# Three banks for single heads' scores, three for maxima, and products of values in two groups a tile

## The chip, the cores and the metric

The kernel runs on one core of one Trainium2 chip. The core has five engines that run their own instruction streams and meet only at semaphores: TensorE (PE, with its weight loads listed as PEld), VectorE (DVE), ScalarE (ACT), GpSimd (POOL) and SyncE (SP), which here issues the DMAs. TensorE writes to the accumulation memory PSUM, eight banks of 128 partitions by 512 float32. The metric is the device time of the whole program in microseconds; lower is better.

## The reference

Four cross-attention layers follow one another. Layer 0 has 16 heads of 64 and a bias; layers 1 to 3, which the change touches, have 16 query heads of 32, four key/value heads shared by four query heads each, and a root-mean-square norm ahead of the queries. Inputs are float32, 8 batches of 512 rows of 512, with 512 context rows of 1024.

```
xn   = x * rsqrt(mean(x*x) + 1e-5) * norm_w
q    = xn @ wq                          # 512 rows, 16 heads of 32
k, v = ctx @ wk, ctx @ wv               # 512 rows, 4 heads of 32
for each head h, with its k and v head g = h // 4:
    p      = softmax(q[h] @ k[g].T / sqrt(32))      # 512 x 512
    o[h]   = p @ v[g]
x    = x + concat(o) @ wo
```

## The kernel before, in words

The program first projects keys and values of all layers, then runs layer 0, then layers 1 to 3 in `grouped_layers`, from about 2150 us to the end. There the work is 24 batches `it` (three layers by eight batches) of four tiles `t`, 96 tiles in all. A tile is one key/value head with its four query heads. For each tile TensorE does the following, by the names used in this text:

- **M0 to M15**, `maximum`, line 2014: 16 products of 128 queries by 512 keys, one bank each, of which DVE takes a row maximum (`reduce_max`, line 1882). They work up to two tiles ahead (`LEAD = 22`). The banks are 4 and 5 in turn, so each waits until the one two before it is reduced.
- **T**, `turn`, line 2036: four transposes that turn the maxima of the next tile, from which ACT writes four rows into the query operand (`shift`, line 1766, in two halves of two instructions).
- **S0 to S7**, `scores`, line 2045: two products each, for two heads (here x.0 and x.1), into banks 0 and 1 or 2 and 3. ACT takes both banks in one instruction (`exponential`, line 1775, here **E0 to E7**) into `probs`.
- **O0 to O3**, `outputs`, line 2059: products of the exponentials with the values, for 128 keys and four heads. Four matmuls of 32 columns each stand side by side in the array; all accumulate in bank 6.
- **D**, `denominators`, lines 2073 and 2078: two sets of the same form with a matrix of ones, in bank 7. POOL adds E2 to E5 to the first ones beforehand (line 1684).
- **Q0 to Q3**, `project_q`, line 2003, and **P0 to P3**, `project_out`, line 2085: three full products each, for the queries three tiles ahead and for the output of the batch before, both in bank 7.

Once a batch, at t = 3, TensorE also sums squares for the batch after next (`sum_squares`, line 1989, here **SS**, bank 7), DVE inverts the mean square and ACT takes its root at t = 1 (`inv_rms`, line 1752, between two table loads).

The order on every engine is written out by hand in its `batch` function, and each engine keeps it. ACT has in every tile E0, rounding of an output, the taking of outputs and denominators, E1, E2, E3, rounding of q, E4, E5, E6, first half of `shift`, E7, second half. TensorE's S0 waits for the first half of `shift`, D for the second (`shifted`). `take_q` (line 1877) is DVE's reading of bank 7 after Q3, between the reductions of M5 and M6; SS and P0 wait for it (`q_taken`). The order of a tile on TensorE stands in the function `batch` below.

Of the kernel before, what the change touches and what calls it, by code (L numbers as in the profile page):

```python
# [5 lines left out]
P = 128  # L6
# [17 lines left out]
KT = S // P  # L24
# [1394 lines left out]
def grouped_layers(nc, name, x_out, k_scratch, v_scratch, wq, wo, shared, norm_w):  # L1419
# [16 lines left out]
    FIRST_TURNB = 3  # L1436

    with ExitStack() as mem:
# [93 lines left out]

        def max_bank(i):
            return 4 + i % 2
# [33 lines left out]
        def _(sp):  # L1568
# [41 lines left out]
            def batch(it, par):  # L1610
# [8 lines left out]
                for t in range(T):  # L1619
                    if there(it, t + AHEAD):  # L1620
                        wait(sp, scored, tile_no(it, t) * NS)
                        load_k(*at(it, t + AHEAD))
                    if there(it, t - LAG):
                        load_residual(it, t)
                    if there(it, t - LAG - 1):
                        store(it, t - 1)
                    if t == 1 and there(it, 2 * T):
                        sp.wait_ge(x_split, (it + 2) * CK)
                        load_x(it + 2)
                    if t == 1 and there(it, T):  # L1630
# [33 lines left out]
        def _(pool):  # L1664
# [14 lines left out]
            def sum_probs(it, t, n):  # L1679
# [3 lines left out]
                pool.wait_ge(exped, g * NS + n + 1)  # L1683
# [43 lines left out]
        def _(act):  # L1727
# [42 lines left out]
            def exponential(it, t, n):  # L1770
                g = tile_no(it, t)
                act.wait_ge(scored, g * NS + n + 1)
                if n < 2:
                    wait(act, summed, (g - 1) * SUMS + n + 1)
                act.activation(probs[:, n], ps[:, 2 * (n % 2):2 * (n % 2) + 2, :], ACT.Exp).then_inc(exped, 1)  # L1775
# [67 lines left out]
        def _(dve):  # L1843
# [41 lines left out]
            def maximum(it, t, i):  # L1885
                t_m, n = max_target(it, t, i)
                if there(it, t_m):
                    reduce_max(tile_no(it, t) * M + LEAD + i, t_m, n, max_bank(i))
# [96 lines left out]
        def _(pe):  # L1985
# [31 lines left out]
            def maximum(it, t, i):  # L2017
                t_m, n = max_target(it, t, i)
                if there(it, t_m):
                    no = tile_no(it, t) * M + LEAD + i  # L2020
                    pe.wait_ge(reduced, no - 1)
                    one_maximum(*at(it, t_m), n, max_bank(i))
# [16 lines left out]
            def scores(it, t, n):  # L2039
# [3 lines left out]
                wait(pe, exped, g * NS + n - 1)  # L2043
                for j in range(2):
                    last = pe.matmul(bank(2 * (n % 2) + j), k_ops[:, s, kt * P:(kt + 1) * P], q_ops[:, s, 2 * hp + j, :],  # L2045
                                     start=True, stop=True)
                last.then_inc(scored, 1)

            def outputs(it, t, kt, par):
# [7 lines left out]
                pe.wait_ge(exped, g * NS + (kt + 1) * (H // 2))  # L2057
# [48 lines left out]
            def batch(it, par):  # L2106
                for t in range(T):
                    scores(it, t, 0)
                    maximum(it, t, 0)
                    outputs(*at(it, t - 1), KT - 1, par if t > 0 else 1 - par)  # L2110
# [14 lines left out]
                    outputs(it, t, 0, par)  # L2125
# [16 lines left out]
                    maximum(it, t, 11)  # L2142
                    outputs(it, t, 1, par)
                    turn(*at(it, t + 1))
                    scores(it, t, 6)
                    maximum(it, t, 12)
# [3 lines left out]
                    outputs(it, t, 2, par)  # L2150
# [7 lines left out]
            for no in range(LEAD):  # L2158
                wait(pe, reduced, no - 1)
                one_maximum(0, no // M, no % M, max_bank(no))  # L2160
                if no == M + 1:
                    pe.wait_ge(reduced, M)
                    for q in range(QT):
# [69 lines left out]
```

## Time and profile before

| what | us |
|---|---|
| median of 3 runs (lowest to highest) | 4220.01 (4219.65 to 4222.34) |
| the profiled execution | 4216.71 |
| its span in the trace | 4214.9 |
| PE busy in the span | 4068.2 |
| DVE busy | 2468.1 |
| ACT busy | 2074.4 |
| first instruction of the 96 tiles' maxima (L2014) | 2172.8 |
| last O of the trace (L2059) | 4195.2 |

All durations in this text are from the one profiled execution. The rows of the timeline give the start and the length of an instruction or of a run of equal ones; on TensorE a matmul is listed for about 0.40 us although the next one starts 0.23 us later, so its pace is read from start to start, and a bracket for idle time shows only what exceeds that overlap. The chain of waits shows each piece with what it adds to the path.

### The profile page before, as it was taken

To read this page: it belongs to the slowest core of one execution; us is meant where nothing else is said; L and a number is where in the kernel's file an instruction comes from. 1 tells how busy PE (TensorE), PEld (TensorE's weight loads), DVE (VectorE), ACT (ScalarE), POOL (GpSimd) and SP (SyncE) were. 2 spreads that over 40 slices of the span, in tenths; PEclk is the share of its full clock that TensorE was granted. 3 is DMA by queue.
4 is the path that set the end of the run, shared out by engine and by line. 5 is a ranking of instruction groups with operands and counts; after the bars stand their busy time and mean duration, and the time that the engine had idled before them with its cause. 6 is when DMAs were issued, how large, how long until landed. Compare 5 with 4: busy or idle time off the path is not lost. (4 is left out here: it accounts for less than half of the span.)

```text
span 4214.9 us, 52271 instructions
## 1 busy us (share of the span) xinstructions
PE 4068.2 (97%) x19496; PEld 2639.1 (63%) x19496; DVE 2468.1 (59%) x3453; ACT 2074.4 (49%) x2648; POOL 2000.2 (47%) x1072
## 2 busy tenths in 40 slices
PE   9999999997999999999969999999999999999999
PEld 7888888885556665666544555555555555555555
DVE  3122300013665556555658778777877887788775
ACT  3111211122444445434427666776676677666665
POOL 0000000003565556555626676667666766676666
PEclk9999999998999999999979999999999999999999
DMA  5333522234455445545533333333333333333322
GB/s 185 130 135 135 173 79 83 88 100 118 131 128 134 122 130 130 133 122 133 128 91 84 88 86 86 96 96 97 83 95 90 86 98 93 94 89 88 93 79 65
DMA packets 316070, 452.01 MB, mean 107 GB/s; under 512 B 45176, under 2 KB 117368, under 8 KB 315832
## 3 DMA queue, kind: packets, MB, share of 16 engines
q1 hardware_dynamic: 315832, 448.86, 37.9%
q8 instruction: 147, 2.41, 0.2%
q14 instruction: 91, 0.75, 0.1%
HBM read 217.72 MB, written 102.77 MB: 76 GB/s over the span
## 5 line engine op out<-in xcount | busy, mean ns | idle before, releaser
L1882 DVE TENSOR_REDUCE a_max_cols<-a_ps 128x1 f32<-128x512 f32 x1536 | 1018.1, 673 | 322.6 <-PE a_ps L2014 316.4
L1775 ACT ACTIVATE a_probs<-a_ps 128x1024 f32<-128x1024 f32 x768 | 784.7, 1025 | 602.7 <-PE a_ps L2045 597.4
L2014 PE MATMUL a_ps<-a_k_ops,a_q_ops 96*128 96x512 f32 x1536 | 652.1, 436 | 50.3 <-DVE a_max_cols L1882 33.3
L1684 POOL TENSOR_TENSOR a_sums<-a_probs 128x1024 f32<-128x1024 f32 x192 | 456.1, 2392 | 321.7 <-ACT a_probs L1775 320.5
L1036 DVE TENSOR_REDUCE a_max_cols<-a_ps 128x1 f32<-128x512 f32 x522 | 346.1, 686 | 342.8 <-PE a_ps L1189 342.8
L2014 PEld LDWEIGHTS a_ps<-a_k_ops,a_q_ops 96*128 96x128 f32 x1536 | 291.3, 190 | 396.4 <-DVE a_max_cols L1882 219.1
L2045 PE MATMUL a_ps<-a_q_ops,a_k_ops 128*128 128x512 f32 x1536 | 492.7, 402 | 1.5 <-ACT a_q_ops L1766 0.9
L803 POOL MEMSET a_ident<- 128x128 f32 x1 | 0.2, 204 | 974.9 <-issue 974.9
L1684 POOL TENSOR_TENSOR a_sums<-a_sums,a_probs 128x1024 f32<-128x1024 f32 x192 | 454.0, 2387 | 0.0
L2059 PE MATMUL a_ps<-a_probs,a_v 128*32 128x512 f32 x3072 | 410.1, 606 | 0.9 <-ACT a_probs L1775 0.9
L303 DVE TENSOR_TENSOR cp_c_lo<-cp_raw,cp_c_hi 128x1024 fp32r<-128x1024 f32 x64 | 78.4, 1225 | 527.7 <-ACT cp_c_hi L247 527.7
L1901 DVE RECIPROCAL a_stage<-a_stage 128x128 f32<-128x128 f32 x384 | 361.2, 942 | 13.7 <-ACT a_stage L1787 13.7
L948 ACT ACTIVATE a_probs<-a_ps 128x1024 f32<-128x1024 f32 x256 | 257.0, 1024 | 142.7 <-PE a_ps L1213 133.1
L2045 PEld LDWEIGHTS a_ps<-a_q_ops,a_k_ops 128*128 128x128 f32 x1536 | 284.0, 190 | 57.4 <-issue 7.2
L826 POOL TENSOR_TENSOR a_sums<-a_sums,a_probs 128x1024 f32<-128x1024 f32 x128 | 311.1, 2430 | 10.0
L1213 PE MATMUL a_ps<-a_q_ops,a_k_ops 128*128 128x512 f32 x1024 | 289.4, 405 | 14.2 <-ACT a_probs L948 13.6
L411 PE MATMUL cp_ps<-cp_w_hi,cp_c_lo 128*128 128x512 f32 (+1 forms) x768 | 285.3, 371 | 0.0
L411 PE MATMUL cp_ps<-cp_w_lo,cp_c_hi 128*128 128x512 f32 (+1 forms) x768 | 285.2, 371 | 0.0
L411 PE MATMUL cp_ps<-cp_w_hi,cp_c_hi 128*128 128x512 f32 (+1 forms) x768 | 285.1, 371 | 0.0
L392 PE MATMUL cp_ps<-cp_c_hi,cp_w_hi 128*128 128x512 f32 x704 | 275.5, 391 | 8.9 <-DVE cp_w_lo L297 8.9
L392 PE MATMUL cp_ps<-cp_c_hi,cp_w_lo 128*128 128x512 f32 x704 | 275.1, 391 | 0.0
L392 PE MATMUL cp_ps<-cp_c_lo,cp_w_hi 128*128 128x512 f32 x704 | 275.1, 391 | 0.0
(131 smaller groups left out, 7182.0 us busy)
## 6 DMA issues: line engine op xcount, KB each, us to landing
a_k_ops<-k_scratch SPq DMA_DIRECT2D x201, 256.0 KB, 4.1
a_q_ops<-a_qn_hi SPq DMA_DIRECT2D x768, 64.0 KB, 2.0
k_scratch<-cp_out SPq DMA_DIRECT2D x88, 512.0 KB, 2.8
a_q_ops<-a_qn_hi SPq DMA_DIRECT2D x268, 128.0 KB, 2.3
cp_raw<-in_ctx_t SPq DMA_DIRECT2D x64, 512.0 KB, 4.1
x_raw<-out_t SPq DMA_DIRECT2D x25, 1024.0 KB, 7.1
a_q_ops<-a_qn_lo SPq DMA_DIRECT2D x384, 64.0 KB, 2.0
a_x_res<-out_t SPq DMA_DIRECT2D x92, 256.0 KB, 3.1
```

What stands on the lines that cost most here:

```text
L392: done = pe.matmul(ps[:, m % BANKS, :], w[:, k, n * P:(n + 1) * P], c[par][:, k, :], start=(k == 0 and i == 0), stop=(k == KC - 1 and i == 2))
L411: done = pe.matmul(ps[:, v_bank(n), 0:w], c[par][:, k, t * P:(t + 1) * P], v[:, k, c0:c0 + w], start=(k == 0 and i == 0), stop=(k == KC - ...
L826: pool.tensor_tensor(sums[:, hp], (probs if i == 1 else sums)[:, hp], probs[:, n], ALU.add)\
L1036: dve.tensor_reduce(max_cols[:, t % 2, col:col + 1], bank(max_bank(p)), AX.X, ALU.max, negate=True).then_inc(reduced, 1)
L1213: last = pe.matmul(bank(2 * (n % 2) + j), k_ops[:, s, k_head(h), p, kt * P:(kt + 1) * P], q_ops[:, s, h, p, :], start=(p == 0), stop=(p == ...
L1684: pool.tensor_tensor(sums[:, hp], (probs if n < H else sums)[:, hp], probs[:, n], ALU.add)\
L1775: act.activation(probs[:, n], ps[:, 2 * (n % 2):2 * (n % 2) + 2, :], ACT.Exp).then_inc(exped, 1)
L1882: dve.tensor_reduce(max_cols[:, t % 2, col:col + 1], bank(b), AX.X, ALU.max, negate=True)\
L1901: dve.reciprocal(part, part).then_inc(recip_done, 1)
L2014: pe.matmul(bank(b), q_ops[0:SHIFT, s, h, q * P:(q + 1) * P], k_ops[0:SHIFT, s, :], start=True, stop=True).then_inc(smax, 1)
L2045: last = pe.matmul(bank(2 * (n % 2) + j), k_ops[:, s, kt * P:(kt + 1) * P], q_ops[:, s, 2 * hp + j, :], start=True, stop=True)
L2059: last = pe.matmul(ps[h * d:(h + 1) * d, OUTB, :], v[:, par, kt, t * d:(t + 1) * d], probs[:, kt * (H // 2) + h // 2, h % 2, :], start=(kt ...
```

## The change

In `grouped_layers` alone:

- The scores of a head go into one of three banks (0 to 2) in turn, head by head. A product of head number i, counted on through the tiles, waits until the exponential of head i - 3 is done. Before, both products of S(n) waited for E(n-2), both heads of it.
- The exponential is one instruction a head (512 columns) in place of one for two heads (1024 columns). `scored` and `exped` count heads.
- The maxima use banks 3, 4 and 5 in turn, so that each waits for the one three before it.
- O2 moves from between M14 and M15 to the next tile, right ahead of O3. O0 moves from between M6 and M7 to right ahead of O1. M12 moves ahead of S6.
- The first turn uses bank 2 and waits for the first queries' taking.

The diff, cut to its core:

```
-    FIRST_TURNB = 3
+    FIRST_TURNB = 2
+    SCORE_BANKS = MAX_BANKS = 3
...
+        def score_bank(g, n, j):
+            return (2 * (g * NS + n) + j) % SCORE_BANKS
         def max_bank(i):
-            return 4 + i % 2
+            return SCORE_BANKS + i % MAX_BANKS
...
             def exponential(it, t, n):
                 g = tile_no(it, t)
-                act.wait_ge(scored, g * NS + n + 1)
                 if n < 2:
                     wait(act, summed, (g - 1) * SUMS + n + 1)
-                act.activation(probs[:, n], ps[:, 2 * (n % 2):2 * (n % 2) + 2, :], ACT.Exp).then_inc(exped, 1)
+                for j in range(2):
+                    act.wait_ge(scored, 2 * (g * NS + n) + j + 1)
+                    act.activation(probs[:, n, j, :], bank(score_bank(g, n, j)), ACT.Exp).then_inc(exped, 1)
...
             def maximum(it, t, i):
-                    pe.wait_ge(reduced, no - 1)
-                    one_maximum(*at(it, t_m), n, max_bank(i))
+                    pe.wait_ge(reduced, no - MAX_BANKS + 1)
+                    one_maximum(*at(it, t_m), n, max_bank(no))
...
             def scores(it, t, n):
-                wait(pe, exped, g * NS + n - 1)
                 for j in range(2):
-                    last = pe.matmul(bank(2 * (n % 2) + j), k_ops[:, s, kt * P:(kt + 1) * P], q_ops[:, s, 2 * hp + j, :],
-                                     start=True, stop=True)
-                last.then_inc(scored, 1)
+                    wait(pe, exped, 2 * (g * NS + n) + j + 1 - SCORE_BANKS)
+                    pe.matmul(bank(score_bank(g, n, j)), k_ops[:, s, kt * P:(kt + 1) * P], q_ops[:, s, 2 * hp + j, :],
+                              start=True, stop=True).then_inc(scored, 1)
...
                     maximum(it, t, 0)
+                    outputs(*at(it, t - 1), KT - 2, par if t > 0 else 1 - par)
                     outputs(*at(it, t - 1), KT - 1, par if t > 0 else 1 - par)
...
                     maximum(it, t, 6)
-                    outputs(it, t, 0, par)
...
                     maximum(it, t, 11)
+                    outputs(it, t, 0, par)
                     outputs(it, t, 1, par)
                     turn(*at(it, t + 1))
+                    maximum(it, t, 12)
                     scores(it, t, 6)
-                    maximum(it, t, 12)
                     maximum(it, t, 13)
                     scores(it, t, 7)
                     maximum(it, t, 14)
-                    outputs(it, t, 2, par)
                     maximum(it, t, 15)
```

Three places show how instructions move. Line numbers of the changed kernel are 5 or 6 higher: L2020 is M, L2051 is S, L2064 is O, L2078 and L2083 are D, L1995 is SS, L1781 is E and L1771 is `shift`.

TensorE, the end of a tile, before: S7, M14, O2, M15, the next tile's S0, M0, O3 and the first set of D.

```order
L2045 MATMUL a_ps<-a_q_ops,a_k_ops 128x512 [waits a1_exped]
L2045 MATMUL a_ps<-a_q_ops,a_k_ops 128x512
L2014 MATMUL a_ps<-a_k_ops,a_q_ops 128x512 [waits a1_reduced]
L2059 MATMUL a_ps<-a_probs,a_v 32x512 [waits a1_exped]
L2059 MATMUL a_ps<-a_probs,a_v 32x512 x3
L2014 MATMUL a_ps<-a_k_ops,a_q_ops 128x512 [waits a1_reduced]
L2045 MATMUL a_ps<-a_q_ops,a_k_ops 128x512 [waits a1_exped,a1_shifted]
L2045 MATMUL a_ps<-a_q_ops,a_k_ops 128x512
L2014 MATMUL a_ps<-a_k_ops,a_q_ops 128x512 [waits a1_reduced]
L2059 MATMUL a_ps<-a_probs,a_v 32x512 [waits a1_exped]
L2059 MATMUL a_ps<-a_probs,a_v 32x512 x3
L2073 MATMUL a_ps<-a_probs,a_ones 32x512 [waits a1_shifted]
```

The same place in the changed kernel: S6, M13, S7, M14, M15, the next tile's S0, M0, O2, O3, the first set of D.

```order
L2051 MATMUL a_ps<-a_q_ops,a_k_ops 128x512 [waits a1_exped] x2
L2020 MATMUL a_ps<-a_k_ops,a_q_ops 128x512 [waits a1_reduced]
L2051 MATMUL a_ps<-a_q_ops,a_k_ops 128x512 [waits a1_exped] x2
L2020 MATMUL a_ps<-a_k_ops,a_q_ops 128x512 [waits a1_reduced] x2
L2051 MATMUL a_ps<-a_q_ops,a_k_ops 128x512 [waits a1_exped,a1_shifted]
L2051 MATMUL a_ps<-a_q_ops,a_k_ops 128x512 [waits a1_exped]
L2020 MATMUL a_ps<-a_k_ops,a_q_ops 128x512 [waits a1_reduced]
L2064 MATMUL a_ps<-a_probs,a_v 32x512 [waits a1_exped]
L2064 MATMUL a_ps<-a_probs,a_v 32x512 x3
L2064 MATMUL a_ps<-a_probs,a_v 32x512 [waits a1_exped]
L2064 MATMUL a_ps<-a_probs,a_v 32x512 x3
L2078 MATMUL a_ps<-a_probs,a_ones 32x512 [waits a1_shifted]
```

Eight full matmuls now stand between the start of S6.0 and S0.1 without a set of O among them, and S0.1 has a wait of its own.

ACT, the end of tile t = 1, before: E4, E5, E6, a half of `shift`, E7, the other half, the next tile's E0.

```order
L1775 ACTIVATE a_probs<-a_ps 128x1024 [waits a1_scored] x3
L1766 ACTIVATE a_q_ops<-a_ps 1x512 [waits a1_turned]
L1766 ACTIVATE a_q_ops<-a_ps 1x512
L1775 ACTIVATE a_probs<-a_ps 128x1024 [waits a1_scored]
L1766 ACTIVATE a_q_ops<-a_ps 1x512 [waits a1_turned]
L1766 ACTIVATE a_q_ops<-a_ps 1x512
L1775 ACTIVATE a_probs<-a_ps 128x1024 [waits a1_summed,a1_scored]
```

The same in the changed kernel.

```order
L1781 ACTIVATE a_probs<-a_ps 128x512 [waits a1_scored] x6
L1771 ACTIVATE a_q_ops<-a_ps 1x512 [waits a1_turned]
L1771 ACTIVATE a_q_ops<-a_ps 1x512
L1781 ACTIVATE a_probs<-a_ps 128x512 [waits a1_scored] x2
L1771 ACTIVATE a_q_ops<-a_ps 1x512 [waits a1_turned]
L1771 ACTIVATE a_q_ops<-a_ps 1x512
L1781 ACTIVATE a_probs<-a_ps 128x512 [waits a1_scored,a1_summed]
L1781 ACTIVATE a_probs<-a_ps 128x512 [waits a1_scored]
```

The order is the same, with two instructions in place of each exponential.

TensorE, the middle of tile t = 3, before: S3, M6, O0, SS, M7.

```order
L2045 MATMUL a_ps<-a_q_ops,a_k_ops 128x512 [waits a1_exped]
L2045 MATMUL a_ps<-a_q_ops,a_k_ops 128x512
L2014 MATMUL a_ps<-a_k_ops,a_q_ops 128x512 [waits a1_reduced]
L2059 MATMUL a_ps<-a_probs,a_v 32x512 [waits a1_exped,a1_out_taken]
L2059 MATMUL a_ps<-a_probs,a_v 32x512 x3
L1989 MATMUL a_ps<-a_sq,a_ones 128x512 [waits a1_sq_step,a1_q_taken]
L2014 MATMUL a_ps<-a_k_ops,a_q_ops 128x512 [waits a1_reduced]
```

The same in the changed kernel, and on to S4 and M8.

```order
L2051 MATMUL a_ps<-a_q_ops,a_k_ops 128x512 [waits a1_exped] x2
L2020 MATMUL a_ps<-a_k_ops,a_q_ops 128x512 [waits a1_reduced]
L1995 MATMUL a_ps<-a_sq,a_ones 128x512 [waits a1_sq_step,a1_q_taken]
L2020 MATMUL a_ps<-a_k_ops,a_q_ops 128x512 [waits a1_reduced]
L2051 MATMUL a_ps<-a_q_ops,a_k_ops 128x512 [waits a1_exped] x2
L2020 MATMUL a_ps<-a_k_ops,a_q_ops 128x512 [waits a1_reduced]
```

SS now follows M6 at once. In the 96 tiles ACT issues 1536 exponentials in place of 768; the other engines issue the same instructions as before.

## Rows read from the trace of the kernel before

**Rows 1.** The page: busy us, share of the span and instructions by engine.
```profile
PE 4068.2 (97%) x19496; PEld 2639.1 (63%) x19496; DVE 2468.1 (59%) x3453; ACT 2074.4 (49%) x2648; POOL 2000.2 (47%) x1072
```

**Rows 2.** By window: length, busy us of PE, PEld, DVE, ACT, POOL, granted clock, DMA.
```profile
3116.57:3137.11 20.54, 20.45 (x109) 11.63 (x108) 17.86 (x27) 14.55 (x19) 13.68 (x7) 1.00 0.30 71
...
3158.24:3178.66 20.42, 20.33 (x110) 11.69 (x109) 15.05 (x22) 14.36 (x18) 14.75 (x9) 1.00 0.34 90
```

**Rows 3.** The chain of waits in tile 2: start, length, what.
```profile
3161.11 0.86 PE a_ps L2078 x8
...
3167.51 0.23 PE a_ps L2014
3167.74 1.00 PE a_ps L2059 x8
3168.74 0.43 PE a_ps L2014
```

**Rows 4.** Timeline, end of tile 2: start, length, engine, operation, count, idle before.
```profile
3175.18 0.70 PE L2045 MATMUL a_ps<-a_q_ops,a_k_ops 128*128 128x512 f32 x2
...
3175.92 1.03 ACT L1775 ACTIVATE a_probs<-a_ps 128x1024 f32<-128x1024 f32 x1 [2.49 <-PE a_ps L2045]
...
3176.18 0.63 PE L2045 MATMUL a_ps<-a_q_ops,a_k_ops 128*128 128x512 f32 x2
...
3176.89 0.49 PE L2014 MATMUL a_ps<-a_k_ops,a_q_ops 96*128 96x512 f32 x1
3176.97 1.18 ACT L1766 ACTIVATE a_q_ops<-a_ps 1x512 fp32r<-1x512 f32 x2
...
3177.32 1.07 PE L2059 MATMUL a_ps<-a_probs,a_v 128*32 128x512 f32 x8
...
3178.17 1.02 ACT L1775 ACTIVATE a_probs<-a_ps 128x1024 f32<-128x1024 f32 x1
...
3179.22 1.19 ACT L1766 ACTIVATE a_q_ops<-a_ps 1x512 fp32r<-1x512 f32 x2
...
3180.46 1.07 PE L2073 MATMUL a_ps<-a_probs,a_ones 128*32 128x512 f32 x8
...
3181.35 1.04 PE L2078 MATMUL a_ps<-a_sums,a_ones 128*32 128x512 f32 x8
```

**Rows 5.** Timeline, middle of tile 1.
```profile
3141.83 0.63 PE L2045 MATMUL a_ps<-a_q_ops,a_k_ops 128*128 128x512 f32 x2
...
3143.53 1.28 ACT L1752 ACT_TABLE_LOAD   x1
...
3144.83 0.63 ACT L1752 ACTIVATE a_inv<-a_ms 128x512 f32<-128x512 f32 x1
...
3146.47 0.62 PE L2045 MATMUL a_ps<-a_q_ops,a_k_ops 128*128 128x512 f32 x2
...
3146.77 1.94 ACT L1775 ACTIVATE a_probs<-a_ps 128x1024 f32<-128x1024 f32 x2
```

**Rows 6.** By source line L1743: count, shortest/median/longest ns, first and last start.
```profile
L1743 ACT ACTIVATE x_hi<-x_raw x46: 1046/1048/1057, 2204.5 to 4053.9; 128x1024 fp32r<-128x1024 f32 x46
```

**Rows 7.** By source line L1738, the same columns.
```profile
L1738 ACT ACTIVATE wq_hi<-a_w_raw x12: 617/620/625, 2300.2 to 3645.8; 128x512 fp32r<-128x512 f32 x12
```

**Rows 8.** Timeline, middle of tile 3.
```profile
3187.76 0.39 PE L2014 MATMUL a_ps<-a_k_ops,a_q_ops 96*128 96x512 f32 x1
3187.89 0.67 DVE L1877 TENSOR_TENSOR a_qf<-a_ps,a_inv 128x512 f32<-128x512 f32 x1
...
3189.07 1.13 PE L1989 MATMUL a_ps<-a_sq,a_ones 128*128 128x512 f32 x2
```

**Rows 9.** Timeline, start of tile 1.
```profile
3137.11 0.63 PE L2045 MATMUL a_ps<-a_q_ops,a_k_ops 128*128 128x512 f32 x2
...
3138.34 0.50 PE L2014 MATMUL a_ps<-a_k_ops,a_q_ops 96*128 96x512 f32 x1 [0.60 <-DVE a_max_cols L1882]
```

**Rows 10.** PE's waits: total us, times, longest us.
```profile
PE a_ps L2014 <- DVE a_max_cols L1882: 33.3, 45, 2.6
```

More of the change, by code:

```diff
@@ L1620, in batch @@
                     if there(it, t + AHEAD):
-                        wait(sp, scored, tile_no(it, t) * NS)
+                        wait(sp, scored, 2 * tile_no(it, t) * NS)
                         load_k(*at(it, t + AHEAD))
@@ L1682, in sum_probs @@
                     pool.wait_ge(summed, g * SUMS + n - H + 1)
-                pool.wait_ge(exped, g * NS + n + 1)
+                pool.wait_ge(exped, 2 * (g * NS + n + 1))
                 pool.tensor_tensor(sums[:, hp], (probs if n < H else sums)[:, hp], probs[:, n], ALU.add)\
@@ L1887, in maximum @@
                 if there(it, t_m):
-                    reduce_max(tile_no(it, t) * M + LEAD + i, t_m, n, max_bank(i))
+                    reduce_max(tile_no(it, t) * M + LEAD + i, t_m, n, max_bank(tile_no(it, t) * M + LEAD + i))
             def split_x(n, k):
@@ L2056, in outputs @@
                     wait(pe, out_taken, g)
-                pe.wait_ge(exped, g * NS + (kt + 1) * (H // 2))
+                pe.wait_ge(exped, 2 * (g * NS + (kt + 1) * (H // 2)))
                 for h in range(H):
@@ L2158, in _ @@
             for no in range(LEAD):
-                wait(pe, reduced, no - 1)
+                wait(pe, reduced, no - MAX_BANKS + 1)
                 one_maximum(0, no // M, no % M, max_bank(no))
@@ L2162, in _ @@
                     pe.wait_ge(reduced, M)
+                    pe.wait_ge(q_taken, AHEAD)
                     for q in range(QT):
@@ L2167, in _ @@
             pairs(pe, batch)
+            outputs(N - 1, T - 1, KT - 2, 1)
             outputs(N - 1, T - 1, KT - 1, 1)
             denominators(N - 1, T - 1)
-            pe.wait_ge(exped, G * NS)
+            pe.wait_ge(exped, 2 * G * NS)
             out_part(T - 1, 0, range(T), 0)
```

## The prediction

> **What bounds the kernel now.** I read the page first. PE is busy for 97% of the span, DVE for 59%, ACT for 49% [rows 1]. The busy times by window then show one batch's tiles of the grouped layers: tile 0 takes 20.54 us and tile 2 20.42, with 20.45 and 20.33 us of PE in them, DVE busy 17.86 and 15.05, ACT 14.55 and 14.36, and the granted clock at 1.00, the 2.4 GHz level [rows 2]. So TensorE's own sequence sets the end there. DVE and ACT have room on average, and what matters is where TensorE waits inside a tile, and what its sequence costs apart from the matmuls. The chain of waits shows the second [rows 3]: a set of O between two Ms adds 1.00 us and the M behind it 0.43, where an M elsewhere adds 0.23 and a set that follows one of its own form 0.86. A change from full to narrow matmuls and back thus costs 0.14 + 0.20 = 0.34 us. The timeline of a tile's end shows the first [rows 4]: M14 starts 0.71 us after the second pair of S instead of 0.47, held by DVE, and the O set 0.43 us after it instead of 0.33, since its load was not hidden.
>
> **The change part by part.** The working is done on tile 2 of one batch and carried to the 96 tiles.
>
> 1. Joined sets. Two of four round trips a tile go, the one of O0 and the one of O2: 2 x 0.34 = 0.68 us. O2 and O3 then stand in front of D, as one narrow stretch.
>
> 2. The end of a tile. S6 starts at 3175.18 and D at 3180.46, 5.28 us [rows 4]. In it ACT is a chain: E6 starts at 3175.92, 0.04 us after S6's end, then half of `shift` at 3176.97 (1.18 us), E7 at 3178.17, the other half at 3179.22, and D begins 0.05 us after that. Before, S0 needed E6 and the first half of `shift`, not E7, and O2 and M15 filled the time. Now S0.1 is three heads behind E7.0, and only M13, S7, M14, M15 and S0.0 stand between S6 and it: eight steps of 0.23, 1.87 us. ACT's chain from M12 on, the first after the transposes, where S6 now starts 0.31 us later (S6's first pair: 0.70 less 0.39 [rows 4]): 0.31 + 0.39 (S6.0) + 0.04 + 1.09 (E6, both heads) + 0.02 + 1.18 + 0.02 + 0.60 (E7.0) + 0.05 = 3.70 us. Then S0.1 with an unhidden load 0.34, M0 0.33, O2 0.89 and O3 0.86 (as D's two sets: 3180.46 to 3181.35, and 0.86 [rows 3, 4]) = 2.42. Together 6.12 us where 5.28 stand now: +0.84, in which O2's round trip and M14's wait are already counted as gains. O0's round trip is outside: -0.34. Net +0.50 us a tile, 95 tile ends: +47.5 us. S7.1 waits for E6.0 and S0.0 for the first half of `shift`, both inside this chain. E7.1 and the second half end at 5.4 us of it, ahead of D.
>
> The trace has no exponential of 512 columns. Copies of 1024 and 512 columns take 1.048 and 0.620 us [rows 6, 7], so 512 columns are worth 0.43, and 1.02 - 0.43 = 0.60. Two exponentials in a row take 1.94 us together and so overlap by 0.10 [rows 5]; a pair of halves is 0.49 + 0.60 = 1.09. Bounds: half of 1.02, so the pair at 1.02 and one at 0.51, which takes 0.16 us from each end of a tile (-15 us) and as much from item 3 (-3); or the 0.62 of the copy with no overlap, 1.24 and 0.62, which adds 0.17 (+16) and in item 3 0.2 plus a wait of S4.1 of up to 0.3 (+11). I take 0.60, the nearest row's.
>
> The Trainium skill ("ScalarE: Activation LUTs", "What ACT_TABLE_LOAD costs") gives an ACTIVATE with immediates 186 ns plus 0.833 ns a column and an overlap of 93 ns. By that the half would be 0.61 us and the pair 1.13, an estimate, and the end of a tile 0.05 us later, some 5 us in all. This case's rows show 1.02 for 1024 columns where it would have 1.04, so its fixed part is a little high here. The same section adds about 1.38 us of drain to each table load; by that E2 would start 2.8 us later than the loads alone make it. The trace disagrees, since the instruction behind the 1.28 us load starts 0.02 us after it [rows 5].
>
> 3. Tile 1. After E1 ACT loads a table (1.28 us), takes the root (0.63), and loads the other table (1.28); E2 starts only at 3146.77 [rows 5]. Before, S3 needed E1, and nothing waited. Now S3.1 needs E2.0. From S1 at 3141.83: 0.40 + 0.04 + 1.09 (E1), loads and root with gaps of about 0.05 in all 3.24, E2.0 0.60, 0.05 = 3147.25. S3.1 stood at 3146.70: +0.55, and 0.10 for its unhidden load. +0.65 us in some 20 batches (three layer starts, where another wait hides it, and the last batch, which takes no root, are out): +13 us. S4.1 comes 1.04 us later and E3.0 ends 0.99 us later, so it just passes.
>
> 4. Tile 3. SS waits for `take_q`, which ends at 3187.89 + 0.67 = 3188.56 [rows 8]. Now it follows M6 (3187.76) directly and would start at 3187.99; it starts at 3188.61 instead, 0.62 us late. Before, O0's set covered this; only its round trip was counted as saved. The 22 batches that have it: +13.6 us. P0 waits for the same in other tiles, but 1.2 us after M6 or later, when it is over.
>
> 5. Third bank for maxima. At the start of tile 1 M0 starts 1.23 us after S0, not 0.47, because DVE has the splits of x between its reductions, and the O set after it 0.10 later [rows 9]. M0 now needs only the reduction of M13, which DVE has long done, since S0.1 is late: -0.86 x 23 = -20 us. Of the visible waits of M on DVE, 33.3 us in 45 times [rows 10], about 14 are these; of the other 19, the longest 2.6, the third bank can save the time of one M's spacing each. I take -4, between 0 and -10.
>
> 6. At nothing: one semaphore count more in S and E (the waits are on the matmuls' own instructions); 15% more ACT work, 8 x 0.17 = 1.4 us a tile under about 6 us idle [rows 2]; POOL, which waits for whole pairs as before and whose last sum ends before the turn; SP, whose K loads wait for the same point. If ACT's cover went, each tile would pay up to 1.4 us, but only its chains above are on the path. The prologue's extra wait stands once.
>
> Sum: +47.5 + 13 + 13.6 - 20 - 4 = +50 us. The profiled execution took 4216.7 and becomes 4267; the median of the runs is 3.3 us above that execution, so the runs' median becomes 4270. In words: 65 us of narrow-to-full changes, some 33 of M14's waits and 24 of other DVE waits are saved, and more than that is paid where TensorE now stands at the three-bank limit.
>
> **The rivals.**
>
> A. The waits are covered (the other side, faster). If ACT's chain to S0.1 took no longer than the 1.87 us of matmuls, only gains would be left: joined sets -65, M14's wait and load 0.34 x 95 = -32, D's small wait of about 0.1 -8, M0 and the rest -24, with items 3 and 4 +27: 4118. It turns the sign once the chain to S0.1 is 0.5 us shorter than my 3.70. Against it: `shift` alone is 1.18 us and is unchanged, and with halves at 0.51 the chain is still 3.54. 6%.
>
> B. It balances, 4220: gains of item 5 grow because M12 to M15 run into reductions elsewhere too, or the unhidden loads cost nothing. That needs 0.5 us a tile from waits of which I see 0.34. 8%.
>
> C. ACT is dearer (slower yet): halves do not overlap, because each waits on its own semaphore, and S4.1 waits in tile 1. The upper bound above, 4270 + 27 = 4297. For it: `shift` behind E6 does not overlap (0.02 us of gap). Against: E3 overlaps E2 although it has a wait. 12%.
>
> D. The change does not do what it says: a joined set still costs a full change, and 65 us do not come, 4334. Against it, D's second set at 0.86 us [rows 3]. 2%.
>
> My forecast 72%.
>
> **How the numbers follow.** The forecast's own range is 4250 to 4285, from the lower bound of the exponential and half of the upper. To leave out no more than 2 in 10 it reaches down towards B and up into C: 4236 to 4297. This kernel's measurement tells 0.2%, 8.4 us, from no change. Faster takes A and a part of B: 0.08. Same takes most of B: 0.08. Slower: 0.84.
>
> **What would show it.** In the changed profile: exponentials of 512 columns at 0.60 us; S6 to D at about 5.8 us, and S0's second matmul starting about 0.05 us after an E7.0; tile 1 with S3.1 behind E2.0; SS right behind `take_q`; M0 of tile 1 no longer held by DVE; O sets joined at 0.86; tile 2 at about 20.9 us. It would be wrong if S0.1 is not held by ACT, or if E6 starts earlier than S6.0's end.

## The result, and the profile after

The changed kernel takes 4279.27 us, the median of 4 runs (4276.54 to 4281.31), against 4221.18 us (4219.65 to 4224.85) for the kernel before on the same chip: ratio 1.0134, interval 1.0119 to 1.0149. It is 58 us slower, where the prediction had 50. The profiled execution took 4276.54 us, with a span of 4274.7, 59.8 more than before.

The page of the changed kernel, which answers to [rows 1]: TensorE is busy for a smaller share of a longer span, and ACT has 768 more instructions, the halved exponentials. Further lines of the changed kernel, beside those named above: L1883 is `take_q`, L1888 `reduce_max`, L2042 the transposes T, L2090 the products P.

```profile
PE 4057.1 (95%) x19496; PEld 2657.4 (62%) x19496; DVE 2461.1 (58%) x3453; ACT 2113.5 (49%) x3416; POOL 1997.1 (47%) x1072
```

The waits of PE in the changed kernel (total us, times, longest), which answer to [rows 10]. The row of M on DVE that led before (33.3 us, 45 times) has shrunk to 5.2, and what leads now is S0 waiting for `shift`:

```profile
PE a_ps L2051 <- ACT a_q_ops L1771: 69.0, 95, 1.2
PE a_ps L2051 <- ACT a_probs L1781: 16.3, 29, 1.8
...
PE a_ps L1995 <- DVE a_qf L1883: 10.3, 22, 0.5
...
PE a_ps L2020 <- DVE a_max_cols L1888: 5.2, 8, 1.7
```

The count is the thing to see: 95 times, once at each tile's end, 22 for SS, once a batch. By window, the four tiles of one batch after (from one S0 to the next; columns as in [rows 2]):

```profile
3225.73:3246.84 21.11, 20.27 (x108) 11.84 (x108) 17.55 (x27) 14.93 (x27) 13.25 (x7) 1.00 0.26 66
3246.84:3268.51 21.67, 20.37 (x109) 11.86 (x109) 17.84 (x27) 16.14 (x28) 12.11 (x7) 1.00 0.45 124
3268.51:3289.41 20.90, 20.06 (x108) 11.93 (x109) 14.76 (x23) 14.73 (x26) 14.52 (x9) 1.00 0.32 80
3289.41:3312.09 22.68, 21.36 (x110) 12.23 (x111) 15.85 (x24) 13.16 (x25) 17.11 (x11) 1.00 0.28 72
```

Tiles 0 and 2 were 20.54 and 20.42 [rows 2]. The clock is 1.00 in all four, so nothing of what these tiles lose is the clock's. (From 2250 us to the last batch the trace of the changed kernel has two short stretches at 0.50, at 2302 and at 2998 us, and that of the kernel before has none; by the 1.7 us that such a stretch costs in a run further down, they are worth some 3 us.) Medians over 20 batches each (batches 3 to 22, start of S0 to start of S0), worked out from the starts of all matmuls in both traces:

| tile | before | after | difference |
|---|---|---|---|
| 0 | 20.54 | 21.13 | +0.58 |
| 1 | 21.14 | 21.66 | +0.52 |
| 2 | 20.41 | 20.91 | +0.50 |
| 3 | 21.45 | 22.68 | +1.23 |

Together +2.83 a batch, 68 over 24 batches. Some 8 us of it do not come, mostly in the first two batches, which differ by -1.8 and +1.5 us.

The end of tile 2 in the timeline of the changed kernel, which answers to [rows 4]:

```profile
3286.31 0.48 PE L2020 MATMUL a_ps<-a_k_ops,a_q_ops 96*128 96x512 f32 x1
...
3286.63 0.64 PE L2051 MATMUL a_ps<-a_q_ops,a_k_ops 128*128 128x512 f32 x2
...
3287.07 1.08 ACT L1781 ACTIVATE a_probs<-a_ps 128x512 f32<-128x512 f32 x2 [2.95 <-PE a_ps L2051]
...
3288.18 1.18 ACT L1771 ACTIVATE a_q_ops<-a_ps 1x512 fp32r<-1x512 f32 x2
...
3289.38 1.09 ACT L1781 ACTIVATE a_probs<-a_ps 128x512 f32<-128x512 f32 x2
...
3289.41 1.13 PE L2051 MATMUL a_ps<-a_q_ops,a_k_ops 128*128 128x512 f32 x2 [0.72 <-ACT a_q_ops L1771]
...
3290.70 1.92 PE L2064 MATMUL a_ps<-a_probs,a_v 128*32 128x512 f32 x16
...
3292.45 1.04 PE L2078 MATMUL a_ps<-a_probs,a_ones 128*32 128x512 f32 x8
```

Read it from the back. O2 and O3 are one run of 16 (1.92). S0's two matmuls take 1.13 us together instead of 0.63, since the second waits for E7.0. S0 starts at 3289.41, 0.05 us after the first half of `shift` ends at 3289.36, where TensorE would have been ready 0.9 us earlier. From M12 to D are 6.14 us. The chain of waits of that tile says the same in pieces:

```profile
3286.79 0.26 PE a_ps L2051
...
3287.07 1.08 ACT a_probs L1781 x2
...
3288.18 0.58 ACT a_q_ops L1771
...
3288.77 0.59 ACT a_q_ops L1771
...
3289.38 0.61 ACT a_probs L1781
```

In the kernel before, the path of the same tile leaves TensorE once, between S6 and M14, for one reduction:

```profile
3176.15 0.70 DVE a_max_cols L1882
```

In the changed kernel it leaves TensorE at S6.0's end for E6, both instructions of the first half of `shift`, and E7.0, which ends at 3289.99: nearly 3 us at the tile's end.

### The profile page after: what moved, and what is told of

Its sections match the earlier page's. It is cut to its first block, busy times and chain, and to the rows that moved or that the text cites. A ratio compares the mean times of both kernels' runs of the same rounds, so it can differ in the third digit from the quotient of the medians.

```text
span 4274.7 us, 53040 instructions
## 1 busy us (share of the span) xinstructions
PE 4057.1 (95%) x19496; PEld 2657.4 (62%) x19496; DVE 2461.1 (58%) x3453; ACT 2113.5 (49%) x3416; POOL 1997.1 (47%) x1072
## 4 chain that ended last, share of the span: by engine, by line
PE 37%; ACT 9%; DVE 3%; issue 1%; SPq 0%; POOL 0%; DMA 0%; ACTq 0%; DVEq 0%
PE a_ps L2064 8%; PE a_ps L2090 6%; PE a_ps L2020 6%; PE a_ps L2051 6%; ACT a_probs L1781 5%; PE a_ps L2009 4%; ACT a_q_ops L1771 3%; PE a_ps L2083 2%; PE a_ps L2078 2%; PE a_ps L2042 1%; DVE a_max_cols L1888 1%; PE a_ps L1995 1%; ACT L1781 1%; ACT L1757 1%; DVE a_qf L1883 0%
## 5 line engine op out<-in xcount | busy, mean ns | idle before, releaser
L1888 DVE TENSOR_REDUCE a_max_cols<-a_ps 128x1 f32<-128x512 f32 x1536 | 998.3, 671 | 409.8 <-PE a_ps L2020 405.4
L1781 ACT ACTIVATE a_probs<-a_ps 128x512 f32<-128x512 f32 x1536 | 830.6, 598 | 577.6 <-PE a_ps L2051 563.5
L2051 PE MATMUL a_ps<-a_q_ops,a_k_ops 128*128 128x512 f32 x1536 | 555.8, 421 | 96.7 <-ACT a_q_ops L1771 69.0
L2020 PE MATMUL a_ps<-a_k_ops,a_q_ops 96*128 96x512 f32 x1536 | 614.2, 421 | 14.2 <-DMA a_q_ops<-a_qn_hi 8.6
L1036 DVE TENSOR_REDUCE a_max_cols<-a_ps 128x1 f32<-128x512 f32 x522 | 346.1, 686 | 342.9 <-PE a_ps L1189 342.9
L2051 PEld LDWEIGHTS a_ps<-a_q_ops,a_k_ops 128*128 128x128 f32 x1536 | 291.1, 190 | 285.1 <-ACT a_probs L1781 126.0
L2020 PEld LDWEIGHTS a_ps<-a_k_ops,a_q_ops 96*128 96x128 f32 x1536 | 292.9, 191 | 156.7 <-issue 87.7
L2064 PE MATMUL a_ps<-a_probs,a_v 128*32 128x512 f32 x3072 | 370.8, 600 | 0.0
L948 ACT ACTIVATE a_probs<-a_ps 128x1024 f32<-128x1024 f32 x256 | 257.0, 1024 | 142.7 <-PE a_ps L1213 133.2
L1213 PE MATMUL a_ps<-a_q_ops,a_k_ops 128*128 128x512 f32 x1024 | 289.5, 405 | 14.2 <-ACT a_probs L948 13.6
L1704 POOL TENSOR_TENSOR a_a_lo<-a_stage,a_a_hi 128x512 fp32r<-128x512 f32 x96 | 122.3, 1274 | 363.0 <-ACT a_a_hi L1797 363.0
```

Of the source, the lines that this page charges most:

```text
L1036: dve.tensor_reduce(max_cols[:, t % 2, col:col + 1], bank(max_bank(p)), AX.X, ALU.max, negate=True).then_inc(reduced, 1)
L1213: last = pe.matmul(bank(2 * (n % 2) + j), k_ops[:, s, k_head(h), p, kt * P:(kt + 1) * P], q_ops[:, s, h, p, :], start=(p == 0), stop=(p == ...
L1781: act.activation(probs[:, n, j, :], bank(score_bank(g, n, j)), ACT.Exp).then_inc(exped, 1)
L1888: dve.tensor_reduce(max_cols[:, t % 2, col:col + 1], bank(b), AX.X, ALU.max, negate=True)\
L2020: pe.matmul(bank(b), q_ops[0:SHIFT, s, h, q * P:(q + 1) * P], k_ops[0:SHIFT, s, :], start=True, stop=True).then_inc(smax, 1)
L2051: pe.matmul(bank(score_bank(g, n, j)), k_ops[:, s, kt * P:(kt + 1) * P], q_ops[:, s, 2 * hp + j, :], start=True, stop=True).then_inc(score ...
```

## The experiments

Theory 1 is the account of the prediction: the new order puts TensorE at the three-bank limit behind ACT's chain at the tile's end, and takes the cover away elsewhere. Theory 2, the rival, puts the loss to the number of banks for scores and holds the new order by itself to be a gain. Times are medians of four executions (of nine or ten in three of the runs); the ratio is to the kernel before, measured together with that run.

### The two halves of the change

**Order alone** (the kernel before with its own banks and exponentials, and the changed order on TensorE):

```
                     maximum(it, t, 0)
+                    outputs(*at(it, t - 1), KT - 2, par if t > 0 else 1 - par)
...
                     maximum(it, t, 6)
-                    outputs(it, t, 0, par)
...
                     maximum(it, t, 11)
+                    outputs(it, t, 0, par)
                     outputs(it, t, 1, par)
                     turn(*at(it, t + 1))
+                    maximum(it, t, 12)
                     scores(it, t, 6)
-                    maximum(it, t, 12)
...
                     maximum(it, t, 14)
-                    outputs(it, t, 2, par)
```

> Only the order of the change on TensorE, with the four score banks, two maximum banks and whole exponentials of before. Theory 1 (cover at the tile's end: with O2 gone from there, ACT's chain E6, half of shift stands open): S0.0 waits for the half of shift at 3.25 us after M12, D comes 5.9 us after M12 (6.1 in the changed kernel), no wait of S3 in tile 1, M0 of tile 1 again held by DVE: about 4266 us. Theory 2 (three banks for heads are the cost, joined sets only a gain): the joined sets save 65 us and nothing is lost, about 4160.

Measured: 4324.17 us, ratio 1.0248 [1.0230, 1.0266]. The direction is Theory 1's, and Theory 2 is out. But the size was missed by 58 us. With two banks the order puts Ms close together that O sets kept apart. The timeline in the middle of tile 2 of this kernel (M is L2014 here):

```profile
3303.15 0.77 PE L2014 MATMUL a_ps<-a_k_ops,a_q_ops 96*128 96x512 f32 x2
3303.28 0.68 DVE L1877 TENSOR_TENSOR a_qf<-a_ps,a_inv 128x512 f32<-128x512 f32 x1
...
3303.87 1.97 DVE L1882 TENSOR_REDUCE a_max_cols<-a_ps 128x1 f32<-128x512 f32 x3
...
3304.61 0.50 PE L2014 MATMUL a_ps<-a_k_ops,a_q_ops 96*128 96x512 f32 x1 [0.21 <-DVE a_max_cols L1882]
```

M6 and M7 stand together, DVE has `take_q` ahead of their reductions, and M8 waits for M6's. Over the span this is 64.0 us of M on DVE (131 times) in place of 33.3. Besides, of 20 tiles 1 (batches 3 to 22) ten took 23.4 us and eight 21.7. A stretch at the granted clock 0.50 lies in each of the long ones and in none of the short ones, so it costs 1.7 us. With 13 such stretches from 2250 us to the last batch, 22 us, and the 31 us of M on DVE, this makes some 53 of the 58, an estimate.

**Banks and exponentials alone** (the changed kernel with the order of before):

```
-                    outputs(*at(it, t - 1), KT - 2, par if t > 0 else 1 - par)
...
                     maximum(it, t, 6)
+                    outputs(it, t, 0, par)
...
                     maximum(it, t, 11)
-                    outputs(it, t, 0, par)
                     outputs(it, t, 1, par)
                     turn(*at(it, t + 1))
+                    scores(it, t, 6)
                     maximum(it, t, 12)
-                    scores(it, t, 6)
...
                     maximum(it, t, 14)
+                    outputs(it, t, 2, par)
```

> Only the banks and the exponentials by heads, in the order of before (O0 behind M6, O2 between M14 and M15, M12 behind S6). Theory 1: O2 covers ACT's chain, S0.1 waits no more than 0.05 us, M14's wait and tile 1's M0 wait are gone, S3.1 in tile 1 still waits for E2.0: about 4194 us, less than before. Theory 2: three banks cost wherever S stands, 4240 to 4280.

Measured: 4193.81 us, 0.9937 [0.9919, 0.9955], as forecast. This half makes the kernel faster. A tile's end in its timeline:

```profile
3242.47 0.70 PE L2051 MATMUL a_ps<-a_q_ops,a_k_ops 128*128 128x512 f32 x2
...
3245.63 0.82 PE L2051 MATMUL a_ps<-a_q_ops,a_k_ops 128*128 128x512 f32 x2
...
3247.65 1.06 PE L2078 MATMUL a_ps<-a_probs,a_ones 128*32 128x512 f32 x8
```

S6 to D is 5.18 us; it was 5.28 [rows 4] and is 5.82 in the changed kernel (3286.63 to 3292.45). S0.1 starts 0.31 us after S0.0 here (median), where the pace is 0.23 and the changed kernel has 0.62.

**Which banks.** Three kernels change only the numbers in `SCORE_BANKS, MAX_BANKS`: 4, 2 and 3, 2 in the changed order, and 4, 2 in the order of before.

```
-    SCORE_BANKS = MAX_BANKS = 3
+    SCORE_BANKS, MAX_BANKS = 4, 2
```

> The changed kernel with four banks for heads and two for maxima, all else the same. Theory 1: S0.0's wait for the half of shift stays (3.08 us after M12), only E7.0's wait of 0.3 us goes; S3.1 in tile 1 waits no more (-0.75 a batch), M0 in tile 1 waits for DVE again (+0.9): about 4254 us. Theory 2: the three-bank limit was the cost, about 4160 to 4200.

> The changed kernel with two banks for maxima instead of three (one bank unused). The joined sets covered DVE too: behind M6 and between M14 and M15 five maxima now follow closely. From the run with four and two banks (4337 us) and the limit of three heads, which adds 0.3 us a tile end and 0.75 in tile 1: about 4350 to 4385 us, and a granted clock under 1 in tile 1. Rival (the two-bank runs were slow for another cause, the four banks): about 4300.

> The order of before, with exponentials by heads in four banks and two banks for maxima: of the banks' change only the split of the exponential. Theory 1: the split is worth nothing by itself, about 4218 us; the 27 us of the banks alone are the third bank for maxima (M14's 0.35 us a tile and tile 1's 0.86) less S3.1's wait. Rival: the split itself gains, since E starts one matmul earlier: 4195 to 4205.

| order on TensorE | scores, maxima | us | ratio [interval] |
|---|---|---|---|
| changed | 3, 3 | 4279.27 | 1.0134 [1.0119, 1.0149] |
| changed | 4, 2 | 4336.80 | 1.0270 [1.0251, 1.0288] |
| changed | 3, 2 | 4350.86 | 1.0306 [1.0289, 1.0324] |
| before | 3, 3 | 4193.81 | 0.9937 [0.9919, 0.9955] |
| before | 4, 2 | 4225.65 | 1.0008 [0.9998, 1.0018] |
| before | 4, 2, E not halved (kernel before) | 4221.18 | 1 |

The first was a miss for both theories (4254, and 4160 to 4200): a fourth bank for scores, bought with the third for maxima, makes it slower by 58 us. The other two came out as expected. Halved exponentials alone are worth nothing that can be measured. That is a balance: by the starts of all matmuls tile 0 is 0.84 us longer than in the kernel before, since M15 comes 1.48 us after the last matmul of O2 and not 0.52, and tiles 1, 2 and 3 are 0.37, 0.11 and 0.10 shorter. The third bank for maxima is worth 32 us in the order of before, together with heads in three banks (4225.65 to 4193.81), and 72 in the changed order (4350.86 to 4279.27). The rows do not add up over the orders: order and bank are tied through DVE. The timeline of the 4, 2 kernel at the start of tile 1 shows what the bank covers:

```profile
3281.84 1.81 DVE L1898 TENSOR_TENSOR x_lo<-x_raw,x_hi 128x512 fp32r<-128x512 f32 x1
...
3284.30 0.50 PE L2020 MATMUL a_ps<-a_k_ops,a_q_ops 96*128 96x512 f32 x1 [1.70 <-DVE a_max_cols L1888]
...
3285.51 0.79 PE L2020 MATMUL a_ps<-a_k_ops,a_q_ops 96*128 96x512 f32 x1 [0.24 <-DVE a_max_cols L1888]
...
3286.23 3.15 PE L2064 MATMUL a_ps<-a_probs,a_v 128*32 128x512 f32 x16
```

M15 waits 1.70 us for a reduction behind DVE's splits of x (L1898). And the joined O sets take 3.15 us, not 1.92. The windows of the same kernel (the whole of tile 1, then two pieces of it) show why: the granted clock falls to 0.50, the 1.2 GHz level, in the first piece, by its mean of 0.68 about 1.3 us before the piece's end. M0, which starts just then and is listed with 0.79 us and not 0.50, and the O sets behind it run at that level.

```profile
3284.64:3307.69 23.05, 22.00 (x109) 12.07 (x107) 17.36 (x27) 15.42 (x27) 11.59 (x6) 0.93 0.37 110
3284.64:3286.64 2.00, 1.76 (x8) 0.68 (x10) 2.00 (x5) 1.94 (x5) 0.00 (x0) 0.68 0.48 115
3286.64:3288.64 2.00, 2.00 (x12) 0.39 (x8) 1.21 (x3) 1.07 (x3) 0.85 (x1) 0.50 0.57 151
```

From 2250 us to the last batch the lower level was granted for some 78 us in the 4, 2 kernel, in the order-alone kernel for some 44 and in the 3, 2 kernel for some 31. At the 1.7 us of a stretch that the order-alone kernel showed, this is an estimated 39, 22 and 15 us.

### The terms of the sum, one by one

Each takes the changed kernel and undoes one thing.

**O2 back** between M14 and M15:

```
-                    outputs(*at(it, t - 1), KT - 2, par if t > 0 else 1 - par)
...
                     maximum(it, t, 14)
+                    outputs(it, t, 2, par)
```

> The changed kernel with O2 alone put back between M14 and M15; it costs a round trip of 0.34 us a tile. Theory 1: the set fills the wait, S0.1 at 3.72 us after M12 hardly waits, D is held by the second half of shift at 5.4 us instead of 6.1: -0.7 a tile, about 4211 us. Theory 2 (the end of a tile was not held by ACT): +0.34 a tile, about 4310.

Measured: 4210.45 us, 0.9975 [0.9965, 0.9985], as forecast. Tile 2 takes 20.22 in place of 20.91. This one move of eight narrow matmuls is 69 us, more than the whole loss.

**The first half of `shift` ahead of E6:**

```
-                    exponential(it, t, 6)
                     if there(it, t + 1):
                         shift(*at(it, t + 1), 0)
+                    exponential(it, t, 6)
                     exponential(it, t, 7)
```

> The changed kernel with the first half of shift ahead of E6 on ACT, TensorE's order kept. Theory 1: the two instructions of shift run while M12 and S6 do, E6 follows; S7.1 waits for E6.0 until 2.1 us after M12, S0.0 and S0.1 run without a wait, S0.1 at 3.2 instead of 3.7, D at 5.5 instead of 6.1: -0.64 us a tile, about 4218 us. Theory 2: ACT's chain has the same length, so nothing moves, 4279.

Measured: 4218.01 us, 0.9995 [0.9985, 1.0004], as forecast. S0's wait is gone, and a part of it turns up at S7.1, 1.12 us behind S7.0. PE's waits show only the move, since 85.1 is what 69.0 and 16.3 were together above:

```profile
PE a_ps L2051 <- ACT a_probs L1781: 85.1, 122, 1.8
```

The gain shows from start to start: S0.0 comes 0.23 us after M15 and not 1.12, S0.1 0.23 after S0.0 and not 0.62, M0 0.27 after it and not 0.34, against S7.1 with 1.12 in place of 0.38. That is 0.61 us a tile.

**O0 back** behind M6 in tile 3 alone:

```
                     maximum(it, t, 6)
+                    if t == T - 1:
+                        outputs(it, t, 0, par)
...
                     maximum(it, t, 11)
-                    outputs(it, t, 0, par)
+                    if t < T - 1:
+                        outputs(it, t, 0, par)
```

> The changed kernel with O0 behind M6 again in the last tile of a batch alone, ahead of SS. Theory 1: SS's wait for take_q (0.62 us, 22 batches) goes and 0.2 of the joined set's saving with it: -0.4 x 22 = -9 us, about 4270. Rival: DVE's mean square only moves and P0 waits for it instead: 4279 or above.

Measured: 4267.64 us, 1.0112 [1.0095, 1.0128], 11.6 less than the changed kernel; tile 3 is 22.27 in place of 22.68.

**No root in tile 1**: a copy in its place, and so no table loads. This kernel leaves the inverse norm out, so only its time means anything.

```
-                act.activation(inv[:, :], ms[:, 1, :], ACT.Sqrt, ...)
+                act.activation(inv[:, :], ms[:, 1, :], ACT.Copy, ...)
```

> The changed kernel with a copy in place of the square root, so that no table is loaded (the inverse norm is not computed; the time alone is read). Theory 1: E2 in tile 1 is at its usual place and S3.1 does not wait: -0.78 x 21 = -16 us, about 4263. Rival: the time is hidden behind later waits, 4279.

Measured: 4257.09 us, 1.0094 [1.0077, 1.0110], 22 less than the changed kernel where 16 were expected; tile 1 is 20.91 in place of 21.66. The excess lies elsewhere: between the profiled executions (20.4 us) 3.1 us lie ahead of the stage's first M (2170.5 against 2173.6 us), in code that the two kernels share, and the stage itself is 17.3 us shorter.

### Better versions

**O2 and M12 back everywhere, O0 back in tile 3:** only O0 and O1 stay joined, in tiles 0 to 2.

> What theory 1 makes of it: three and three banks, O2 between M14 and M15, M12 behind S6, O0 joined with O1 except in the last tile of a batch. D 5.10 us after S6 instead of 5.28 before, O0's round trip saved in three tiles of four, tile 1's M0 wait gone, S3.1's wait there: about 4175 us, 1.1% less than before. Rival (joined sets give nothing net): 4194 as for the banks alone, or more.

Measured: 4181.12 us, 0.9916 [0.9899, 0.9932], 6 above the forecast. Tile 2 takes 19.98. S0.1 still comes 0.32 us after S0.0, and D starts 0.56 us after the last matmul of O3 where 0.41 is the least, both behind ACT.

**The same with S6 ahead of the transposes:**

```
                     outputs(it, t, 1, par)
+                    scores(it, t, 6)
                     turn(*at(it, t + 1))
-                    scores(it, t, 6)
```

> The best order so far (4181 us: O2 between M14 and M15, M12 behind S6, O0 joined in three tiles of four) with S6 ahead of the transposes. Theory 1: E6 runs during them, the chain E6, shift, E7 starts 0.4 us earlier, S0.1 and D wait no more: 5.34 us from the place of the transposes to D instead of 5.51: -0.2 a tile, about 4162 us. Rival: ACT's total of the tile's end sets it, 4181.

Measured: 4151.94 us, 0.9838 [0.9821, 0.9854], 10 better than forecast. It beats both kernels, by 69 and by 127 us. The end of tile 2 in its timeline:

```profile
3217.06 1.08 ACT L1781 ACTIVATE a_probs<-a_ps 128x512 f32<-128x512 f32 x2 [2.31 <-PE a_ps L2051]
3217.09 0.60 PE L2042 MATMUL a_ps<-a_ident,a_max_cols 128*128 128x128 f32 x4
...
3218.80 1.06 PE L2064 MATMUL a_ps<-a_probs,a_v 128*32 128x512 f32 x8
...
3220.13 0.63 PE L2051 MATMUL a_ps<-a_q_ops,a_k_ops 128*128 128x512 f32 x2
```

E6 runs beside the transposes, O2 beside `shift`, and S0's pair is back at 0.63, with no wait. In the window of tile 2 the length and PE's busy time are the same number:

```profile
3200.48:3220.13 19.65, 19.65 (x109) 11.84 (x108) 14.68 (x22) 14.73 (x26) 14.54 (x9) 1.00 0.33 85
```

**S6 ahead of O0, with O2 still beside O3**, and O0 back behind M6 in tile 3:

```
                     maximum(it, t, 6)
+                    if t == T - 1:
+                        outputs(it, t, 0, par)
...
                     maximum(it, t, 11)
-                    outputs(it, t, 0, par)
+                    scores(it, t, 6)
+                    if t < T - 1:
+                        outputs(it, t, 0, par)
                     outputs(it, t, 1, par)
                     turn(*at(it, t + 1))
                     maximum(it, t, 12)
-                    scores(it, t, 6)
```

> The changed kernel's joined sets (O2 and O3 ahead of D) with S6 ahead of O0 and O1, O0 alone behind M6 in the last tile of a batch. Theory 1: E6 is done before the transposes, shift follows them at once and E7.0 ends 2.1 us after M12, so S0.1 waits 0.3 us instead of 1.9: 5.2 us to D where the changed kernel takes 6.5 from the transposes; S6.1 waits up to 0.5 for E5.0 in tile 2 behind the squares. About 4150 us. Rival: S6 only moves its wait forward to E5, 4180 or more.

Measured: 4172.83 us, 0.9884 [0.9868, 0.9901], 23 above the forecast. S0.1 comes 0.54 us after S0.0. The timeline shows what starts ACT's chain now:

```profile
3212.60 1.09 ACT L1781 ACTIVATE a_probs<-a_ps 128x512 f32<-128x512 f32 x2 [1.25 <-PE a_ps L2051]
...
3214.58 0.66 PE L2042 MATMUL a_ps<-a_ident,a_max_cols 128*128 128x128 f32 x4
...
3215.28 1.18 ACT L1771 ACTIVATE a_q_ops<-a_ps 1x512 fp32r<-1x512 f32 x2 [1.59 <-PE a_ps L2042]
```

E6 is out of the way early, and ACT then idles 1.59 us for the transposes. From these on, `shift` and E7.0 (0.70 + 1.18 + 0.02 + 0.60 = 2.50 us) are longer than the matmuls up to S0.1, with no O2 among them. Of the two covers, S6 early and O2 late, one is not enough.

## Why the prediction was right, and where it was off

**Joined sets (item 1): right.** The chain of waits of the changed kernel has O2 and O3 together, and D's sets behind them without a change:

```profile
3269.86 1.85 PE a_ps L2064 x16
3271.71 0.86 PE a_ps L2078 x8
```

1.85 is 1.00 + 0.86 less 0.01, with the parts of [rows 3]. Inside the stretch each four matmuls start 0.43 us after the four before (0.45 the first time), through O2, O3 and D alike, and rival D (a joined set costs a full change) is out. The Trainium skill ("TensorEngine Tiling (Array Packing)", "Key Properties") says that changing the tiling mode drains TensorE. The traces agree: 0.34 us for a change to narrow and back in [rows 3], and none between O3 and D.

**The end of a tile (item 2): right.** Forecast from M12 to D 6.12 us, measured 6.14; forecast for a tile's end +0.50 net, measured +0.50 in tile 2, for which the forecast had no other term. The exponentials are what they were taken for (one group of the instructions by line: busy us and mean ns, then idle us before them and for what):

```profile
L1781 ACT ACTIVATE a_probs<-a_ps 128x512 f32<-128x512 f32 x1536 | 830.6, 598 | 577.6 <-PE a_ps L2051 563.5
```

0.60 each, 1.08 to 1.09 for a pair. Rival C's 0.62 without overlap is out, and so is A: the chain is not covered. B needed 0.5 us a tile more from the waits of M, which fell by 0.3 a tile in all (33.3 to 5.2 us). The two runs that change the chain (O2 back, `shift` first) came out at the forecast time within 1 us. That O2's cover was lost at this point is therefore shown, not only argued.

**Tile 1 (item 3): right mechanism, mis-sized.** The timeline, which answers to [rows 5]:

```profile
3252.05 0.64 PE L2051 MATMUL a_ps<-a_q_ops,a_k_ops 128*128 128x512 f32 x2
...
3256.70 0.39 PE L2051 MATMUL a_ps<-a_q_ops,a_k_ops 128*128 128x512 f32 x1
...
3256.89 2.07 ACT L1781 ACTIVATE a_probs<-a_ps 128x512 f32<-128x512 f32 x4
...
3257.54 0.50 PE L2051 MATMUL a_ps<-a_q_ops,a_k_ops 128*128 128x512 f32 x1 [0.45 <-ACT a_probs L1781]
```

S3.1 starts 5.49 us after S1; 5.42 were forecast. On the mean over batches it stands 0.91 us behind S3.0 instead of 0.23, and its load costs 0.10: 0.78 where 0.65 was forecast, +2.6 us over 20 batches. The run without the root shortens the stage by 17 us, where the term was forecast at 13.

**Tile 3 (item 4): right, with a saving counted too high.** The timeline, which answers to [rows 8]:

```profile
3299.73 0.39 PE L2020 MATMUL a_ps<-a_k_ops,a_q_ops 96*128 96x512 f32 x1
3299.86 0.68 DVE L1883 TENSOR_TENSOR a_qf<-a_ps,a_inv 128x512 f32<-128x512 f32 x1
3300.59 1.12 PE L1995 MATMUL a_ps<-a_sq,a_ones 128*128 128x512 f32 x2 [0.47 <-DVE a_qf L1883]
```

SS starts 0.86 us after M6, 0.63 more than the pace (forecast 0.62). But O0's removal saves only 0.22 us in this tile, not 0.34, because the load behind SS stays unhidden: about +2.5 us. The sum of both, 0.41 a batch, is what the run with O0 back in tile 3 regains.

**P0 (item 4): wrong for tile 0.** The prediction let P0 wait for nothing, because it comes "1.2 us after M6 or later, when it is over". In tile 0 of the changed kernel it was not:

```profile
3236.54 0.68 DVE L1883 TENSOR_TENSOR a_qf<-a_ps,a_inv 128x512 f32<-128x512 f32 x1
...
3237.36 0.47 PE L2090 MATMUL a_ps<-a_a_hi,wq_hi 128*128 128x512 f32 x1
```

`take_q` ends at 3237.22 and P0 starts 0.14 after it, as it does in the median of the batches. The profile names no releaser for this start, so that `take_q` holds it is argued: from this closeness, from P0's wait for `q_taken`, and from the kernel before, where `take_q` ended 1.3 us ahead of P0. In the kernel before, O0's set stood between M6 and M7 and P0 followed M8 after 0.24; now it follows after 0.36, and its second matmul 0.31 later and not 0.23: 0.20 us, +5 us. I had placed the wait by the end of `take_q` in tile 3 alone. In tile 0 it sits later in DVE's queue, and the set that was moved away had covered two waiters, not one.

**Third bank (item 5): right, with the saving in tile 1 counted too high.** M0 of tile 1 follows S0.1 after 0.34 us (3247.47 to 3247.81), the pace and the unhidden load and nothing more. But the forecast took 0.86 us for it and overlooked D. In the other tiles of the kernel before, D waits for `shift` and starts 1.00 us after O3 does (3179.53 and 3180.52 in the chain of waits of tile 2). In its tile 1, where M0 came late, `shift` was long done:

```profile
3138.78 1.06 PE L2059 MATMUL a_ps<-a_probs,a_v 128*32 128x512 f32 x8
...
3139.66 0.61 PE L2073 MATMUL a_ps<-a_probs,a_ones 128*32 128x512 f32 x4
```

D follows after 0.88 there, so that only 0.74 of the 0.86 was to be won: +2.8 us over 23 batches. The waits of M on DVE fell by 28 us, from 33.3 to 5.2, where the forecast counted 14 + 4. What the prediction did not see is what the bank would be worth in other orders (32 and 72 us), because it asked only for waits visible before.

Tile by tile the forecast comes to +0.50, +0.29 (0.50 + 0.65 - 0.86), +0.50 and +1.12 us, and the table above has +0.58, +0.52, +0.50 and +1.23. The excess of 0.08, 0.23 and 0.11, by 24, 20 and 22 tiles, makes some 9 us, against the 10 by which the span's +59.8 exceeds the forecast's +50. That tile 0 misses by so little is luck. P0's 0.20 was partly made up at M5: in the kernel before, this M started 0.25 us after the matmul before it, held by DVE, and the next one 0.34 behind it, while with the third bank both run at 0.23 or so, 0.13 us less together. The forecast had neither.

The loss by order of 85 us (4193.81 to 4279.27) splits as follows: O2's move 69, O0's in tile 3 12 (both run by themselves), M12 ahead of S6 about 17 (4210.45 to 4181.12, less those 12), and O0's move in tiles 0 to 2 about -13 (4193.81 to 4181.12), the only one that pays. The last two are differences of runs that changed more than one thing, so they hold only if the moves add up.

## What to carry to other kernels

A narrow matmul set between full ones looks like overhead (0.34 us a round trip here), but it may be what keeps TensorE busy while another engine's chain runs. Before moving it, write down every instruction behind the old place that waits for another engine, in every tile, and price the shortest cover that is left. When a buffer ring gets shallower, join only sets in places with nothing to cover; then move the producer of the critical chain (here S6) forward instead, which gave 4151.94 us where the joined order gave 4279.27.

## What the runs showed of the hardware that was not expected

- The granted clock can fall within a tile after short stalls. In the 4, 2 kernel M15 had waited 1.70 us and M0 0.24, with single full matmuls between, and at the narrow sets that followed the clock was at 0.50. Each four matmuls then started 0.84 to 0.86 us after the four before instead of 0.43, and 0.93 of full clock over 23.05 us is 1.6 us lost in that tile, close to the 1.7 of the order-alone kernel. In the changed kernel all four windows shown stand at 1.00. That the stall is the cause was not tried by itself.
- A split of x on DVE (L1898, 128x512) takes 0.68 us, but 1.81 in the one at 3281.84 of the 4, 2 kernel, beside POOL's multiply of 1.27 us at 3281.82. All 92 splits of a trace say the same: with no POOL instruction beside them none takes more than 0.68 us (46 of them in the changed kernel, 50 in the 4, 2 kernel); the 46 others of the changed kernel take 0.81 to 2.25 us, most of them 1.15 to 1.25. No run moved POOL's work by itself.
- A matmul that had to wait costs 0.10 us more in what follows it, since the next load was not hidden: M0 0.34 after S0.1 instead of 0.23. Each new wait on TensorE is to be priced with it.
- The Trainium skill's formula for an exponential ("ScalarE: Activation LUTs", "What ACT_TABLE_LOAD costs": 186 ns and 0.833 a column, 93 ns of overlap) gives 0.61 us for 512 columns, an estimate. Measured: 0.60 (the mean above), and 0.10 of overlap (2 x 0.60 less 1.09).
